# Two attention layers and a mixture of experts on one core: queries, keys and value sums kept in DRAM, and exponentials of two heads in one instruction

## What is computed

```python
# block 1: causal attention with ALiBi, 16 heads of 8 channels
def _L0_attn_ref(x, ...):
    q = (x @ Wq + bq)...; k = (x @ Wk + bk)...; v = (x @ Wv + bv)...
    scores = jnp.einsum('bqhd,bkhd->bhqk', q, k) * scale
    scores = scores + alibi_slopes(H)[:, None, None] * pos
    scores = jnp.where(causal, scores, -jnp.inf)
    out = jnp.einsum('bhqk,bhkd->bhqd', softmax(scores), v)
    return out.reshape(B, T, C) @ Wo + bo
# block 2: full attention, then 8 experts, two per token, hidden width 512
def _L0_ffn_ref(x, ...):
    x = x + _layernorm(_attention(x, ...), ln1_g, ln1_b)
    return x + _layernorm(_moe(x, ...), ln2_g, ln2_b)
x = x + _layernorm(_L0_attn_ref(_layernorm(x), ...))
x = x + _layernorm(_L0_ffn_ref(_layernorm(x), ...))
```

## Time and profile before

| what | value |
|---|---|
| median of 3 timed runs | 2152.36 us (2148.48 to 2157.9) |
| profiled execution, its own time | 2156.67 us |
| its span in the trace | 2154.9 us |
| mean granted TensorE clock | 0.920 of full speed |
| PE, VectorE (DVE), ScalarE (ACT), GpSimd (POOL) busy | 86%, 77%, 60%, 23% of the span |
| transfers | 50.79 MB, mean 24 GB/s |

### The profile page before, as it was taken

The page is one execution under the profiler, slowest core; times in us unless marked ns, Lnnn a source line. Parts: engine busy times, 40 slices in busy tenths (PEclk is TensorE's granted clock), DMA queues, the critical chain, the costliest instruction groups (busy, mean ns, idle before and its releaser), DMA issues. The chain is left out here.

```text
span 2154.9 us, 40102 instructions
## 1 busy us (share of the span) xinstructions
PE 1852.5 (86%) x10684; PEld 1005.3 (47%) x10684; DVE 1654.5 (77%) x3192; ACT 1286.4 (60%) x2549; POOL 489.2 (23%) x469
## 2 busy tenths in 40 slices
PE   5299999999996479998999899999946999999996
PEld 3155545455535334433343344333314666666664
DVE  5288878788835578888888788888515998998886
ACT  5136666676665406776777677777744665555563
POOL 5201112111113500000000000000014556665554
PEclk8569999999987658999999999999977999999998
DMA  2121111111002120111111111110021000000000
GB/s 70 20 43 29 24 28 28 22 29 30 3 1 79 44 42 13 19 21 21 16 19 16 17 16 16 16 16 1 1 65 34 21 21 21 20 20 1 20 11 10
DMA packets 40481, 50.79 MB, mean 24 GB/s; under 512 B 9128, under 2 KB 27696, under 8 KB 40256
## 3 DMA queue, kind: packets, MB, share of 16 engines
q1 hardware_dynamic: 38880, 47.81, 11.6%
q10 hardware_dynamic: 1376, 0.33, 0.1%
HBM read 14.29 MB, written 6.29 MB: 10 GB/s over the span
## 5 line engine op out<-in xcount | busy, mean ns | idle before, releaser
L411 ACT ACTIVATE at_probs<-at_b 128x512 f32<-128x512 f32 (+3 forms) x1792 | 874.1, 556 | 496.0 <-PE at_b L362 489.5
L439 DVE TENSOR_REDUCE at_mx<-at_a 128x1 f32<-128x512 f32 (+3 forms) x1664 | 995.1, 662 | 211.4 <-PE at_a L334 130.5
L362 PE MATMUL at_b<-at_fqm,km 64*128 64x512 f32 (+3 forms) x1792 | 624.9, 446 | 50.6 <-ACT at_probs L411 30.8
L334 PE MATMUL at_a<-km,fq 64*128 64x512 f32 (+2 forms) x1664 | 507.7, 462 | 84.3 <-DMA km<-packed_k_hi 57.8
L362 PEld LDWEIGHTS at_b<-at_fqm,km 64*128 64x128 f32 x1792 | 293.6, 189 | 498.1 <-ACT at_probs L411 421.7
L379 PE MATMUL at_pv<-at_probs,at_vst 128*32 128x512 f32 (+3 forms) x3584 | 446.2, 571 | 0.0
L334 PEld LDWEIGHTS at_a<-km,fq 64*128 64x128 f32 x1664 | 251.4, 194 | 176.9 <-DVE at_mx L439 94.6
L1181 ACT ACTIVATE t_hid<-t_bank_h,b1t 128x512 f32<-128x512 f32 x256 | 174.1, 689 | 199.6 <-DVE t_hid_lo L1315 115.4
L1315 DVE TENSOR_TENSOR t_hid_lo<-t_hid,t_hid_hi 128x512 fp32r<-128x512 f32 x256 | 230.0, 934 | 14.7 <-ACT t_hid_hi L1188 11.7
L516 POOL TENSOR_SCALAR_AFFINE_SELECT at_probs<-at_probs 128x512 f32<-128x512 f32 x128 | 81.6, 637 | 472.9 <-ACT at_probs L411 472.9
L499 POOL COPY at_vst<-tokens 128x256 f32 (+1 forms) x32 | 12.8, 401 | 745.5 <-PE at_pv L379 745.4
(11 more groups left out here) (223 smaller groups left out, 1924.8 us busy)
## 6 DMA issues: line engine op xcount, KB each, us to landing
fq<-packed_q_hi SPq DMA_DIRECT2D x256, 32.0 KB
km<-packed_k_hi SPq DMA_DIRECT2D x256, 32.0 KB
km<-packed_k_lo SPq DMA_DIRECT2D x128, 32.0 KB
fq<-packed_q_lo SPq DMA_DIRECT2D x128, 32.0 KB
t_raw<-L_ffn_W SPq DMA_DIRECT2D x16, 256.0 KB, 3.1
x_first<-L_attn_x SPq DMA_DIRECT2D x4, 512.0 KB, 7.5
second_x_in<-L_attn_x SPq DMA_DIRECT2D x8, 256.0 KB, 3.2
kept<-second_joined SPq DMA_DIRECT2D x8, 256.0 KB, 2.4
```

What stands on the lines that cost most here:

```text
L334: mm = pe.matmul(scores, fq[g][rows, qt * P:(qt + 1) * P], km[g][rows, first:first + k, kh * HALF:kh * HALF + w], start=True, stop=not dia ...
L362: mm = pe.matmul(out[:, 0:w], km[g][rows, j % 2, kt * P:(kt + 1) * P], fqm[g % 2][rows, q0:q0 + w], start=True, stop=True)
L411: act.activation(probs[t % PROBS][:, j, 0:w], b_bank[n % B_BANKS][:, 0:w], ACT.Exp).then_inc(exp_done, 1)
L439: dve.tensor_reduce(mx[:, kh, qt, heads[0]:heads[0] + k], scores[:, 0:k * w].rearrange("p (k w) -> p k w", k=k), AX.X, ALU.max).then_inc(a ...
```

## The change

Queries and keys are no longer kept in SBUF. Each group of a pass writes its split parts to DRAM tensors `query` and `key` by six transfers of 256 KB (`put`), the constant rows are written there once by four transfers (`fills`, about 6 MB in all, DRAM to DRAM), and a slot is loaded by `load_slot` in five transfers: 512 KB into `fq` and 4 x 112 KB into `km`. The first three slots are loaded inside the pass, right behind the puts of its second group, where SP first waits for puts, fills and each slot before.

The value sums go to DRAM (`sums`, 2 x 256 KB a slot) as they are; `otr` and its VectorE steps go. The denominators are inverted in bulk, and `heads_t` in the second pass and in the tail is one GpSimd product of sums and inverses, loaded by two transfers, in place of four PE transposes and a ScalarE copy.

The maxima are turned by one transpose, copied by VectorE into `m_rows`, and put into four places of `fq` by four small transfers; the adds into `fqm` go.

B gets two buffers of two banks (`b_pair`), and one ScalarE instruction takes the exponentials of two heads. A has three banks in place of four. The order in a step is `b b`, the chunks, `b b`; `m` and `mtr` stand earlier (`MAX_LEAD`), `a_next` is 28 in at2. In the passes the due times are new, the `high` step of the second pass goes from GpSimd to VectorE, and the work that made the constant rows goes.

```diff
-RING = ("a", "otr", "mtr")
-A_BANKS = 4
-B_BANKS = 3
+RING = ("a", "mtr")
+A_BANKS = 3
+B_PAIRS = 2
+FIRST_SLOTS = 3
+MAX_LEAD = 4
...
-        a_steps = nq - 2 - self.lead
-        self.a_next = -(-self.na * 4 // nq)
-        o0 = self.half_end[0] + 1
-        self.o_steps = (o0, nq - 1)
-        self.mt_steps = (a_steps, a_steps + 1)
+        a_steps = nq - self.lead - MAX_LEAD
+        self.a_next = -(-self.na * (nq - a_steps) // nq)
         self.m_step = a_steps - 1
...
-            out += bs[:1] + ass + bs[1:]
+            out += bs[:2] + ass + bs[2:]
...
+def load_slot(sp, loaded, query, key, b, g, fq, km):
+
+    sp.dma_start(fq[g][:, :].bitcast(F32),
+                 query[bass.ds(b * 1, 1), g * GH:(g + 1) * GH, :, :]).then_inc(loaded, 16)
+    for j in range(GH):
+        sp.dma_start(km[g][HW * j:HW * j + KEY_ROWS, j % 2, :].bitcast(F32),
+                     key[bass.ds(b * 1, 1), g * GH + j, :, :]).then_inc(loaded, 16)
...
-                        act.activation(probs[t % PROBS][:, j, 0:w], b_bank[n % B_BANKS][:, 0:w],
+                        act.activation(probs[t % PROBS][:, j:j + 3:2, 0:w], b_pair[n // 2 % B_PAIRS][:, :, 0:w],
                                        ACT.Exp).then_inc(exp_done, 1)
...
+                        dve.tensor_copy(m_rows[:, :], misc[0:2 * GH * TB, 0:P]).then_inc(m_read, 1)
...
+                        for j in range(GH):
+                            row = HW * j + ROW_MAX
+                            sp.dma_start(fq[g][row:row + 2, :].bitcast(F32),
+                                         m_rows[2 * TB * j:2 * TB * (j + 1), :]).then_inc(m_landed, 16)
+                    elif what == "oev":
+                        done(sp, o_read, 2, s, n)
+                        done(sp, o_put[n], 16, s - 1, 15)
+                        sp.dma_start(sums[bass.ds(b * 1, 1), g, :, n * HALF:(n + 1) * HALF],
+                                     osb[:, n, :]).then_inc(o_put[n], 16)
...
+                    if n == 1:
+                        for p in put:
+                            sp.wait_ge(p, PUTS)
+                        extra.get("filled", lambda _: None)(sp)
+                        for g in range(FIRST_SLOTS):
+                            sp.wait_ge(loaded, LOADS * (g + 1))
+                            load_slot(sp, loaded, query, key, 0, g, fq, km)
...
+                elif step == "heads_t":
+                    after(pool, "pe", "project", n - 2)
+                    pool.wait_ge(heads_landed[n % 2], 32 * (n // 2 + 1))
+                    pool.tensor_tensor(heads_t[n % 2][:, :], num_in[n % 2][:, :], inv_in[n % 2][:, :],
+                                       ALU.mult).then_inc(made["pool", step], 1)
```

More of the change, by code:

```diff
@@ L148, in prologue @@
     def prologue(self):
-        out = [("load", s, 0) for s in range(3)]
-        out += [("a", 0, c) for c in range(self.na)]
-        out += [("m", 0, 0), ("mtr", 0, 0), ("mtr", 0, 1)]
+        out = [("a", 0, c) for c in range(self.na)]
+        out += [("m", 0, 0), ("mtr", 0, 0)]
         bs = [("b", 0, i) for i in range(GH * self.lead)]
@@ L298, in bank_free @@
                 def bank_free(step):
-                    place = places[step] - A_BANKS
-                    while True:
-                        back = 0 if place >= 0 else 1
-                        if prologue and back:
-                            return
-                        what, ds, n = held[place]
-                        if held[place] in emitted[back]:
-                            break
-                        place -= A_BANKS
+                    bank = places[step] % A_BANKS
+                    earlier = [(0, k) for k in range(places[step]) if k % A_BANKS == bank]
+                    if not prologue:
+                        earlier = [(1, k) for k in range(len(held)) if k % A_BANKS == bank] + earlier
+                    earlier = [(back, held[k]) for back, k in earlier if held[k] in emitted[back]]
+                    if not earlier:
+                        return
+                    back, (what, ds, n) = earlier[-1]
                     s = s0 + (ds - back)
@@ L564 @@
+    "pool": {"k_hi": 3.34, "k_lo": 3.52},
+    "sp": {"put": 0},
 }
 SPLIT_OFF = {
[L566 to L574 removed]
+    "pe": {"turn": 4.76, "values": 5.66, "k": 5.95, "q": 6.35},
@@ L605, in rows_pass @@
         out = {k: [sb(f"{k}_out{i}", [P, HALF]) for i in range(2)] for k in "qk"}
+        split = {(m, k): [sb(f"{m}_{k}{i}", [P, HALF], F32R) for i in range(2)] for m in "qk" for k in ("hi", "lo")}
+        put = [sem(f"put{i}") for i in range(2)]
         turned32 = [sb(f"turned32_{i}", [P, HALF]) for i in range(2)]
@@ new lines, in _ @@
+            if join:
+                sp.dma_start(den[:, :], dens[B - 1]).then_inc(den_landed, 16)
+            extra.get("sync", lambda _: None)(sp)
+            for step, n in order("sp"):
+                i = n % 2
+                if step == "heads_in":
+                    if n == GROUPS - 2:
+                        sp.wait_ge(inverted, 1)
+                        sp.dma_start(inverses[B - 1].rearrange("h (c t) -> (h c) t", t=P),
+                                     inverse[:, :]).then_inc(inverse_put, 16)
+                    after(sp, "pool", "heads_t", n - 2)
+                    load_heads(n)
+                elif step == "x_in":
+                    after(sp, "pool", "x1", n - 2)
+                    sp.dma_start(x_in[i][:, :, :], group(x, n)).then_inc(x_landed[i], 16)
+                elif step == "kept":
@@ L651, in _ @@
+            for p in put:
+                sp.wait_ge(p, PUTS * GROUPS // 2)
+            if join:
                 for s in kept_landed + kept_u_landed:
@@ L658, in _ @@
                 i = n % 2
[L659 to L664 removed]
+                if step == "project":
+                    after(pe, "pool", "heads_t", n)
                     after(pe, "dve", "y", n - 2)
```

433 lines of the change are left out of this document (219 added, 214 removed).

## The result

The changed kernel takes 2191.06 us (median of 4, 2182.38 to 2198.83) against 2151.28 us before (median of 4): 1.018 times the time before, 95% interval 1.013 to 1.022. It is slower by some 40 us; the forecast was 2140 us and faster by some 0.5%. The time lies outside the forecast's own range (2115 to 2165), 4 us inside the wide one (2078 to 2195), and on the side that had a chance of .32. The profiled execution is the fastest of the four (2182.38 us, span 2180.7 against 2154.9), so the profiles differ by 26 us where the medians differ by 40.

The account below looks back on a forecast made before the run. It took PE as near its limit in at1 and waits on score banks as at2's limit. Terms +46 - 49 - 8 - 9 + 3.5 + 2 = -14.5 gave 2142 profiled, 2140 us forecast; own range 2115 to 2165, wide 2078 to 2195.

Parts of the forecast that it names:

- The mechanism of at2: In at2, with three chunk banks the fourth chunk waits for the first reduce: slot 51.3 us, stage +46 us.
- Rival (A): In at2, the reduce frees the bank early enough, so chunks do not hold PE up: 2065 us, chance .14.
- The second pass: Before at2, heads arrive by transfer and no load follows the pass: at2 starts at 757 against 765.6, -9 us.
- The passes. First: Before at1, constant-row work and loads go, 21.8 MB move at 321 GB/s: first matmul near 97.5, -8 us.
- rival (B): In the passes, puts and fills move at 190 GB/s, at1 starts at 118 or later: 2195 us, chance .16.
- The share near 1: In the passes, a DMA share near 1 in the profile after would show the prediction wrong.
- at1: less for PE: In at1, fewer transposes on a nearly full PE: slot 28.0 us instead of 31.3, stage -49 us.
- its sign of being wrong: In at1, a slot that stays above 29.5 us would show the prediction wrong.
- Rival (C): In at1, only the transposes or less are gained, three-bank wait falling on PE: slot 29.5, 2160 us, chance .13.
- Ends and tail: Storing, awaiting and loading the last sums +3.5 us; the tail's eight GpSimd products +2 us, between -4 and +13.
- The sum: Whole kernel: all terms together -14.5 us, 2142 us for the profiled execution, 2140 us said for the median.
- Rival (E): In at2, PE's clock falls to its lower level in steps with more idle time: +326 us, chance .06.

## Why the prediction was wrong

The terms that failed are three: at1's slot (28.0 us taken, 29.54 measured), the first pass (-8 taken, +4 measured, because the transfers did not run at the full rate) and the tail (+2 taken, some +10 measured, because one small operation came late). The mechanism of at2 held.

**What held.** at2: the wait of the fourth chunk for the first one's reduce, a step of 3.16 (forecast 3.17 to 3.2), the step with five chunks 3.77 (3.75), a slot of 51.2 (51.3), the stage +41 (+46). The step with `mtr` took 3.13, not 2.85, and steps without chunks 2.0 (1.85). PE's wait for `at_mx` and next to none for the exponentials (17 us in all of at2): as foretold, and the experiments on the banks and the order confirm the reason. Rival (A), no wait, is refuted by the wait of .55 us in the step above. The second pass came out at -7 (-9), but in part by luck: the prediction had SP's block of loads fit "with room", while the run with late loads shows that it delays the puts by 14 us, so the pass without it is shorter than was taken by about as much.

**"The passes. First": -8, measured +4.** This step failed in its reading of SP. It let all 21.8 MB move at 321 GB/s in one stretch, with a block of 15 us for the loads. In the trace the engines were busy .55 from 26 to 61 us: four issues of puts stood 4.2 to 6.7 us each behind the fills, and the loads began at 60.8 only. Moving half the fills took 17.6 us off. The rate itself was fair (75 to 106 us: 307 GB/s at a share of .94), so rival (B)'s slow puts were not the cause, though its place was right. (Its price is also mis-added: the terms that it names, 20, 15 and 10, give 2185, not 2195.) The share near 1, which the prediction named as a sign of being wrong, did come, in the last 31 us.

**"at1: less for PE": -49, measured -26.** The term for the slot was mis-sized: 29.54 instead of 28.0, 22 us over 14.4 slots, and just above the 29.5 that the prediction named as its sign of being wrong. Of the 1.5 us, .9 are masks, which cost 2.1 and not 1.2, and .6 are sums rounded down, as worked out with the run without masks. Rival (C)'s 29.5 was the right number, but not for its reason alone: spreading the chunks, which takes the three-bank wait away, gives 1.2 a slot, and the prediction had that wait in its steps of four. The loop's entry and its changes of batch are also longer than before, by 9.7 us in at1 together. With the 22 this is more than the 23 missed, so the terms for the stage's start and end were too high by some 9 and hide it. Starts of the slot's marker around the first change of batch, after and before:

```profile
L441 DVE TENSOR_TENSOR at_mfull<-at_mx x2: 191/191/191, 259.4 to 297.9; 128x32 f32<-128x32 f32 x2
```

```profile
L447 DVE TENSOR_TENSOR at_mfull<-at_mx x2: 537/537/537, 258.0 to 294.5; 128x32 f32<-128x32 f32 x2
```

38.5 and 36.5: 9.0 and 5.1 more than a slot. In both PE stands ahead of the batch's first instructions (2.33 us after, 2.72 before) and the clock falls. After the change it stays down for some 17 us, before for some 7 (windows, after and before):

```profile
279.00:295.50 16.50, 15.74 (x81) 7.67 (x81) 7.71 (x13) 7.63 (x10) 0.63 (x1) 0.50 0.17 43
```

```profile
274.00:280.00 6.00, 6.00 (x35) 2.73 (x33) 3.92 (x8) 2.96 (x8) 0.64 (x1) 0.50 0.30 44
```

With spread chunks the same change costs 5.2 to 6.0. The prediction has nothing for this. Why the clock stays down longer, no run isolates, and the length differs between executions (6.6 to 11.3 for at2's last one, across the kernels with the changed attention as it is), so it stays open.

**"Ends and tail": +5.5 in all, of which I had some +4 behind at2; measured +13 there.** Some 3.6 of it stand before the first block's marker, near the ends' +3.5; 9.9 are in the seven blocks behind it, where the +2 was. The +2 had the right suspects (GpSimd's product beside VectorE) and missed what stood behind them: `comb_lo`, PE's idle 1.25 us, and the clock. Moving one due time took 14 us off.

**The sum.** 12 + 23 + 10 (second pass, ends and tail together) and 5 back in at2 make the 40 us between -14.5 and +26. The remaining 14 us to the medians' +40 are that the profiled execution was the fastest of four after (8.7 under the median) and stood 5.4 over the median before; forecast and median should be compared with that in mind, since the sum was taken down a little for the very same reason.

Rival (E), the clock falling throughout at2's thinner steps, did not come: .99 from 800 to 1556. It fell in pieces, at the changes of batch and of blocks.

## What to carry to other kernels

When buffers of one ring are given to another, first write down for the ring that shrinks how many instructions stand between a buffer's fill and its refill in the engine's program order, and what one round costs; here one bank less cost 7.4 us a slot in the order of the kernel before, banks, pairs and order together 6.6 in the changed one, and nearly all of that came back by spreading the chunks over the step. Large transfers at the head of a queue can cost more than their bytes (here 17.6 us for what moves in some 10), because what the same engine issues behind them stands; what is not needed soon goes behind what is. And when work is put beside a busy engine, look at the next small operation in that engine's order and at who idles for it: blocks with an idle of 1.25 us took 63.4 to 64.0 us, with the lower clock behind it 65.3, and with neither 62.0 to 62.9. And write a term's sum out to the end: .6 of at1's 1.5 us a slot were lost in rounding.

## What was not expected of the hardware

- Issuing a transfer took .6 us with room in the queue and up to 6.70 us when 6 MB of fills stood ahead.
- GpSimd's product and VectorE's subtraction lengthen each other: 1.74 us against 1.26 in the fastest of the eight products, 3.83 against 2.73 for three subtractions, and 2.73 again in both runs that moved the product away.
- The exponential of 1024 columns in two banks took 1.02 us, less by .18 than two of 512 (.60 each) by duration; four singles follow each other in 2.07, two pairs in 1.94 (run with the spread chunks), so back to back the pair saves only .13 for four heads.
- After stops of 1.2 to 3.1 us in the changed kernel PE's granted clock was .50 for 7 to 17 us, at changes of batch and at four of six turns of blocks. It does not follow from the stop alone: at 404 us in the kernel before PE stood for 2.73 us and the clock from 404 to 412 is 1.00.
